# A four-layer state-space block between two mixtures of experts: small arithmetic off GpSimd, skip term on TensorE, packed expert remainders, one delta buffer

## The reference

```python
def ffn(x):                       # E = 8 experts, F = 344, the best K = 2 of them count
    topk_w, topk_idx = top_k(x @ Ws + bs, 2)
    combine = sum(one_hot(topk_idx, 8) * softmax(topk_w)[..., None], axis=1)
    h = silu(einsum('td,edf->tef', x, Wg)) * einsum('td,edf->tef', x, Wu)
    return einsum('ted,te->td', einsum('tef,efd->ted', h, Wd), combine)

def mamba_block(x, p):            # 256 inner channels d, 16 states s
    xp, z = split(rmsnorm(x, p.norm_w) @ p.Win)
    xc = silu(causal_depthwise_conv(xp, p.conv_w, p.conv_b))     # 4 taps
    dt, Bm, Cm = split(xc @ p.Wx)
    delta = softplus(dt @ p.Wdt + p.bdt)
    h[t] = exp(delta[t] * A) * h[t-1] + delta[t] * xc[t] * Bm[t]  # for each d, s
    y = sum_s(h * Cm) + xc * p.Dp                                 # the skip term is xc * Dp
    return x + (y * silu(z)) @ p.Wblk

x = x + 0.5 * ffn(layernorm(x))                                   # "FFN of kind 1"
x = x + (four mamba_blocks of layernorm(x)) @ Wout + bout
x = x + 0.5 * ffn(layernorm(x))                                   # "FFN of kind 2"
```

## Time and profile before

| | |
|---|---|
| time, median of 3 runs | 4565.08 us (4559.62 to 4566.4) |
| profiled execution, first to last instruction | 4554.2 us; no time beyond this span is given for it, and the median is 10.9 us more |
| POOL busy | 4093.5 us (90%) |
| DVE busy | 4047.9 us (89%) |
| PE busy | 3939.2 us (86%), mean granted clock 0.951 |
| ACT busy | 3342.2 us (73%) |
| chain that ended last | POOL 41%, issue 16%, DVE 14%, PE 12%, ACT 8%, DMA 3% |

### The profile page before, as it was taken

One profiled execution on the slowest core, in us unless ns is written; L12 is line 12 of the kernel. 1 busy time (PEld: TensorE's weight loads), 2 busy tenths in 40 slices (PEclk: granted clock), 3 DMA queues, 4 the chain that ended last, 5 costly groups with the idle time before them and its releaser, 6 DMA issues.

```text
span 4554.2 us, 48397 instructions
## 1 busy us (share of the span) xinstructions
PE 3939.2 (86%) x11712; PEld 1280.3 (28%) x11712; DVE 4047.9 (89%) x5505; ACT 3342.2 (73%) x5047; POOL 4093.5 (90%) x1804
## 2 busy tenths in 40 slices
PE   7886777998999999899998999999899989678769
PEld 2221222232322323232232323223232323122223
DVE  2668898999999999999999999999999999889963
ACT  4566776777777777777778777777777777667734
POOL 0559999999999999999999999999999999999960
PEclk9897887999999999999999999999999999789969
DMA  2233544354434444544454445444444554444410
GB/s 72 61 78 95 115 106 98 85 118 110 97 87 112 107 93 99 114 104 96 98 112 96 97 101 119 95 97 101 112 92 89 117 113 91 101 99 95 99 41 5
DMA packets 154562, 434.46 MB, mean 95 GB/s; under 512 B 16429, under 2 KB 53230, under 8 KB 153903
## 3 DMA queue, kind: packets, MB, share of 16 engines
q1 hardware_dynamic: 154287, 431.36, 41.4%
HBM read 150.28 MB, written 12.58 MB: 36 GB/s over the span
## 4 chain that ended last, share of the span: by engine, by line
POOL 41%; issue 16%; DVE 14%; PE 12%; ACT 8%; DMA 3%; SPq 2%; DVEq 0%; ACTq 0%; POOLq 0%
POOL work L909 21%; POOL work L900 19%; DVE work L720 5%; DVE dA_ps L720 4%; SPq L363 2%; PE d_ps L434 2%; PE s_ps L481 2%; DVE work L725 2%; DMA bc_sb<-bc_rows 2%; ACT sg_sb L583 2%; ACT L583 1%; PE b_ps L427 1%; ACT dA_ps L556 1%; DMA dd_sb<-dd_src 1%; ACT L584 1%
## 5 line engine op out<-in xcount | busy, mean ns | idle before, releaser
L909 POOL TENSOR_TENSOR work<-dd_sb,bc_sb 128x2048 f32<-128x2048 f32 x512 | 2319.6, 4531 | 72.4 <-DMA dd_sb<-dd_src 72.2
L556 ACT ACTIVATE dA_ps<-dd_sb,a_sb 128x512 f32<-128x512 f32 x2048 | 1369.2, 684 | 643.1 <-DVE work L725 542.9
L900 POOL TENSOR_TENSOR work<-work,bc_sb 128x1024 f32<-128x1024 f32 x704 | 1655.9, 2359 | 35.1 <-DVE work L720 34.7
L720 DVE TENSOR_TENSOR_SCAN work<-dA_ps,work 128x512 f32<-128x512 f32 x1408 | 1646.7, 1203 | 40.7 <-POOL work L909 32.0
L720 DVE TENSOR_TENSOR_SCAN dA_ps<-dA_ps,work 128x512 f32<-128x512 f32 x640 | 780.9, 1220 | 10.9 <-ACT dA_ps L556 5.1
L434 PE MATMUL d_ps<-sg_sb,wd_sb 128*128 128x512 f32 (+1 forms) x1536 | 721.0, 601 | 18.8 <-DVE sg_sb L805 18.8
L405 PE MATMUL y_ps<-work,sel_sum 128*32 128x512 f32 x4096 | 580.3, 640 | 81.9 <-POOL work L900 53.7
L421 PE MATMUL a_ps<-xT_sb,wg_sb 128*128 128x512 f32 (+1 forms) x768 | 439.5, 655 | 87.1 <-ACT sg_sb L583 80.7
L421 PE MATMUL b_ps<-xT_sb,wg_sb 128*128 128x512 f32 (+1 forms) x768 | 434.5, 648 | 92.2 <-ACT sg_sb L583 87.8
L725 DVE TENSOR_TENSOR work<-dA_ps,bc_sb 128x512 f32<-128x512 f32 x640 | 435.8, 681 | 8.3
L427 PE MATMUL a_ps<-xs_sb,wu_sb 128*128 128x512 f32 (+1 forms) x768 | 412.2, 619 | 20.7 <-DVE sg_sb L805 16.2
(11 more groups left out here) (116 smaller groups left out, 3823.6 us busy)
## 6 DMA issues: line engine op xcount, KB each, us to landing
dd_sb<-dd_src SPq DMA_DIRECT2D x512, 512.0 KB, 8.5
bc_sb<-bc_rows SPq DMA_DIRECT2D x256, 512.0 KB, 5.8
xr_sb<-in_L_attn_x SPq DMA_DIRECT2D x16, 256.0 KB, 3.3
bc_rows<-dbc_sb SPq DMA_DIRECT2D x128, 32.0 KB, 1.7
x<-xr_sb SPq DMA_DIRECT2D x16, 256.0 KB, 3.6
xr_sb<-x SPq DMA_DIRECT2D x16, 256.0 KB, 2.9
out<-xr_sb SPq DMA_DIRECT2D x16, 256.0 KB, 2.3
wg_sb<-in_L_ffn_Wg SPq DMA_DIRECT2D x1, 1376.0 KB
```

Source lines behind the costliest of these rows:

```text
L556: act.activation(dA_ps[:, g % NDA, :], dd_sb[:, b, c, 0, :], ACT.Exp, scale=a_sb[:, l, b, j, c:c + 1]).then_inc(dA_ready, 1)
L720: dve.tensor_tensor_scan(dA if on_dve(i) else tile, dA, tile, 0.0, ALU.mult, ALU.add).then_inc(scanned, 1)
L900: pool.tensor_tensor(work[:, g % RING], work[:, g % RING], bc_sb[:, j, 0, :].unsqueeze(1).broadcast_to([128, 2, T]), ALU.mult).then_inc(po ...
L909: pool.tensor_tensor(work[:, g % RING:g % RING + 2].rearrange("p h c t -> p (h c) t"), dd_sb[:, b, :, 1, :], bc_sb[:, j, 1, :].unsqueeze(1 ...
```

## The change

- **POOL** keeps `dbu` and products only. The layernorm's power becomes Ln and Exp on ACT, and the rest of the small arithmetic goes to DVE. `bn_sb`, `mv_sb` and `rs_sb` become double.
- **`DVE_UNITS`** has six units in place of five, so DVE makes 12 products a phase and POOL 10 pairs in place of 11.
- **The skip term** becomes a matmul of `xc` with a diagonal matrix `ddiag_sb`, the first to write `y_ps` for its half. `y_sb` goes; the product with silu(z) is written over `zs_sb`.
- **Expert remainders.** The last 88 rows of F of four experts, padded to 96, lie together in three tiles. Experts 0 and 4 have two tiles and the others three, 22 to an FFN in place of 24. `xs_sb` becomes double, and `u` of a packed tile is four matmuls of 32 columns.
- **`dd_src`** has one buffer for both halves. `sp1` (the Abs of `b` = 1) waits for the landing of the four DMAs of `b` = 0, and `sp0` for those of `b` = 1 of the phase before.
- **All tables** have other ticks.

```diff
-FT = [(0, 128), (128, 128), (256, 88)]
-NFT = len(FT)
+PACK, PIECE = 4, 32
+NFT, GT = 3, 11
...
-CORE = {"exp": -10, "scan": -1, "dbu": -3, "dve_prod": 0, "pool_prod": 21, "sum": 30, "y0": 87, "y1": 8}
-PREP = {"dc1": 79, "dc0": 65, "sq": -15, "ms": -10, "rms": -10, "xn": 2, "xp0": 15, "conv0": 17, "xp1": 25, "conv1": 25,
-        "silu_xc": 27, "z0": 35, "zc0": 27, "z1": 44, "zc1": 43, "silu_z": 59, "wx": 41, "dbc": 40, "rows": 4, "dt0": 48,
-        "sp0": 48, "delta0": 55, "du0": 59, "dt1": 75, "sp1": 72, "delta1": 79, "du1": 82, "dd0": 49, "dd1": 86, "bc": 52}
-NEAR = {"dc1": 98, "dc0": 84, "sq": 14, "ms": 25, "rms": 24, "xn": 27, "xp0": 45, "conv0": 42, "xp1": 47, "conv1": 53,
-        "silu_xc": 59, "z0": 69, "zc0": 60, "z1": 72, "zc1": 67, "silu_z": 91, "wx": 76, "dbc": 75, "rows": 48, "dt0": 77,
-        "sp0": 77, "delta0": 84, "du0": 84, "dt1": 84, "sp1": 86, "delta1": 93, "du1": 101, "dd0": 71, "dd1": 109, "bc": 55}
-POST = {"x1": 8, "wblk": 83, "h": 91, "attn": 105, "x2": 105}
-POST_NEAR = {"x1": -65, "wblk": 17, "h": 14, "attn": 35, "x2": 56}
-FFN_AT = {"gb": 5, "xs": 2, "g0": 5, "g1": 10, "g2": 10, "burst": 5, "u0": 10, "u1": 17, "u2": 21, "hh0": 13, "hh1": 16,
-          "hh2": 21, "down": 28}
-START = {"load": -130, "bn": -60, "nb": -44, "xtok": -54, "xt": -38, "xT": -47, "lg": -32, "lg_sb": -35, "mx": -32,
-         "mi": -28, "gap": -17, "we": -31, "eq": -27, "den": -17, "inv": -27, "comb": -13, "ct": -12, "gates": -19}
-END = {"yt": 21, "xo": 32, "bn": 41, "nb": 62, "xtok": 61, "ht": 84, "h": 74, "store": 133, "acc": 10}
+CORE = {"exp": -9, "scan": -1, "dbu": -24, "dve_prod": 2, "pool_prod": 11, "sum": 31, "y0": 90, "y1": 9}
+PREP = {"dc1": 84, "dc0": 51, "sq": -15, "ms": -6, "rms": -8, "xn": 3, "xp0": 17, "conv0": 13, "xp1": 21, "conv1": 22,
+        "silu_xc": 27, "z0": 101, "zc0": 96, "z1": 112, "zc1": 105, "silu_z": 123, "wx": 35, "dbc": 36, "rows": 25, "dt0": 38,
+        "sp0": 40, "delta0": 47, "du0": 52, "dt1": 67, "sp1": 77, "delta1": 82, "du1": 84, "dd0": 11, "dd1": 112, "bc": 71}
+NEAR = {"dc1": 103, "dc0": 78, "sq": 9, "ms": 24, "rms": 19, "xn": 27, "xp0": 46, "conv0": 46, "xp1": 55, "conv1": 54,
+        "silu_xc": 59, "z0": 120, "zc0": 111, "z1": 121, "zc1": 117, "silu_z": 123, "wx": 65, "dbc": 61, "rows": -6, "dt0": 67,
+        "sp0": 69, "delta0": 76, "du0": 76, "dt1": 93, "sp1": 96, "delta1": 106, "du1": 107, "dd0": 45, "dd1": 117, "bc": 65}
+POST = {"x1": 37, "wblk": 92, "h": 93, "attn": 108, "x2": 106}
+POST_NEAR = {"x1": -37, "wblk": 15, "h": 11, "attn": 60, "x2": 59}
+FFN_AT = {"gb": 6, "xs": 4, "g0": 5, "g1": 8, "g2": 10, "burst": 5, "u0": 11, "u1": 13, "u2": 16, "hh0": 13, "hh1": 15,
+          "hh2": 21, "down": 34}
+START = {"load": -130, "bn": -50, "ln": -53, "rs": -52, "nb": -45, "xtok": -47, "xt": -37, "xT": -42, "lg": -37, "lg_sb": -34, "mx": -34,
+         "gap": -34, "mi": -34, "we": -36, "eq": -33, "den": -34, "inv": -34, "w1": -33, "eqw": -30, "comb": -28, "hi": -27,
+         "rest": -24, "mid": -20, "lo": -19, "ct": -14, "gates": -23}
+END = {"yt": 36, "xo": 35, "bn": 37, "ln": 39, "rs": 39, "nb": 49, "xtok": 58, "ht": 81, "h": 78, "store": 133, "acc": 3}
...
-DVE_UNITS = (0, 2, 3, 5, 6)
+DVE_UNITS = (0, 1, 3, 5, 6, 7)
...
+def tiles_of(e):
+    return range(0 if e % PACK else 1, NFT)
+def tiles_until(x):
+    return GT * (x // PACK) + max(0, NFT * (x % PACK) - 1)
+def tile_number(x, ft):
+    return tiles_until(x) + (ft if x % PACK else ft - 1)
+def owner(e, c):
+    return e - e % PACK + (4 * (e % PACK - 1) + c) // 3
 def job_bank(x, job):
-    return "ab"[(7 * x + job) % 2]
+    return "ab"[(2 * tiles_until(x) + x + job) % 2]
...
+        ddiag_sb = sb("ddiag_sb", [128, NL, NBLK, 128])
...
-        dd_src = sb("dd_src", [128, NBLK, 2, T])
+        dd_src = sb("dd_src", [128, 2, T])
...
-        xs_sb = sb("xs_sb", [128, T])
+        xs_sb = sb("xs_sb", [128, 2, T])
...
+                    if j == 0:
+                        pe.wait_ge(xc_ready, 2 * k + b + 1)
+                        pe.matmul(y_ps[:, :], ddiag_sb[:, PHASE[w][1], b, :], xc_sb[:, w % 2, b, :],
+                                  start=True, stop=False).then_inc(y_skip, 1)
                     for c in range(NG):
                         g = HALVES * k + 2 * u + c // 2
                         last = pe.matmul(y_ps[SEL * c:SEL * (c + 1), :], sel_sum[:, :], work[:, g % RING, c % 2, :],
-                                         start=(j == 0), stop=(j == NJ - 1))
+                                         start=False, stop=(j == NJ - 1))
                     last.then_inc(summed, 1)
...
+                    if (at := EXPERT_OF.get(t - FFN_AT[f"u{ft}"])) and ft in tiles_of(at[1]):
                         f, e = at
-                        ps = fill(job_bank(E * f + e, 4 + ft), hh_ready, NFT * (E * f + e) + ft + 1)
-                        pe.wait_ge(xs_ready, E * f + e + 1)
-                        pe.matmul(ps[0:fn, :], wu_sb[:, e, f0:f0 + fn], xs_sb[:, :], start=True, stop=True).then_inc(u_full, 1)
+                        x = E * f + e
+                        ps = fill(job_bank(x, u_job(x, ft)), hh_ready, tile_number(x, ft) + 1)
+                        pe.wait_ge(xs_ready, x + 1)
+                        if ft == 0:
+                            for c in range(NG):
+                                last = pe.matmul(ps[PIECE * c:PIECE * (c + 1), :],
+                                                 wu_sb[:, tile_number(e, ft), PIECE * c:PIECE * (c + 1)],
+                                                 xs_sb[:, owner(e, c) % 2, :], start=True, stop=True)
+                            last.then_inc(u_full, 1)
+                        else:
+                            pe.matmul(ps[:, :], wu_sb[:, tile_number(e, ft), :], xs_sb[:, e % 2, :], start=True, stop=True).then_inc(u_full, 1)
...
+                    for ft in tiles_of(e):
+                        pe.wait_ge(hh_ready, tile_number(E * f + e, ft) + 1)
+                        last = pe.matmul(d_ps[:, :], wd_sb[:, tile_number(e, ft), :], sg_sb[:, ft, :], start=(tile_number(e, ft) == 0),
...
+            def log_act(what, f):
+                m = NORM_OF[what, f]
+                act.wait_ge(mv_done, m + 1)
+                if m > 1:
+                    act.wait_ge(xtok_ready, m - 1)
+                act.activation(rs_sb[:, m % 2, 0, :], mv_sb[:, m % 2, :, 1], ACT.Ln, bias=eps_sb[:, 0:1]).then_inc(var_log, 1)
+
+            def rstd_act(what, f):
+                m = NORM_OF[what, f]
+                act.wait_ge(var_log, m + 1)
+                act.activation(rs_sb[:, m % 2, 0, :], rs_sb[:, m % 2, 0, :], ACT.Exp, scale=-0.5).then_inc(rstd_done, 1)
...
-                            act.wait_ge(y_gated, 2 * (before - 1) + b + 1)
+                            act.wait_ge(wblk_full, before)
...
-                        if k > 0:
-                            act.wait_ge(dd_loaded[b], 64 * k)
-                        act.activation(dd_src[:, b, 0, :], s_ps[:, :], ACT.Abs).then_inc(sp_abs, 1)
+                        if b == 1:
+                            act.wait_ge(dd_loaded[0], 64 * (k + 1))
+                        elif k > 0:
+                            act.wait_ge(dd_loaded[1], 64 * k)
+                        act.activation(dd_src[:, 0, :], s_ps[:, :], ACT.Abs).then_inc(sp_abs, 1)
...
-                    par, l = w % 2, PHASE[w][1]
+                    par = w % 2
                     dve.wait_ge(summed, UNITS * k + NJ * (b + 1))
-                    dve.scalar_tensor_tensor(y_ps[:, :], xc_sb[:, par, b, :], dp_sb[:, l, b:b + 1], y_ps[:, :],
-                                             ALU.mult, ALU.add).then_inc(y_skip, 1)
-                    dve.wait_ge(y_skip, 2 * k + b + 1)
                     dve.wait_ge(zs_ready, 2 * k + b + 1)
-                    if k > 0:
-                        dve.wait_ge(wblk_full, k)
-                    dve.tensor_tensor(y_sb[:, b, :], zs_sb[:, par, b, :], y_ps[:, :], ALU.mult).then_inc(y_gated, 1)
+                    dve.tensor_tensor(zs_sb[:, par, b, :], zs_sb[:, par, b, :], y_ps[:, :], ALU.mult).then_inc(y_gated, 1)
...
+                    if xn > 1:
+                        dve.wait_ge(u_full, tile_number(xn - 1, 1))
+                    dve.tensor_tensor(xs_sb[:, e % 2, :], xT_sb[:, f % 2, :], ps_of[job_bank(xn, 0)][:, :], ALU.mult).then_inc(xs_ready, 1)
...
+                dve.scalar_tensor_tensor(rs_sb[:, m % 2, 1, :], mv_sb[:, m % 2, :, 0], -1.0, rs_sb[:, m % 2, 0, :], ALU.mult, ALU.mult).then_inc(nb_ready, 1)
...
+                if (f := UNIT_OF.get(t - START["gap"])) is not None:
+                    dve.wait_ge(mx_ready, f + 1)
+                    if f > 0:
+                        dve.wait_ge(we_ready, f)
+                    dve.tensor_tensor(wt_sb[:, 0, :], mx_sb[:, :, 1], mx_sb[:, :, 0], ALU.subtract).then_inc(gap_ready, 1)
...
+                if (f := UNIT_OF.get(t - START["eqw"])) is not None:
+                    dve.wait_ge(rt_step, 4 * f + 3)
+                    dve.wait_ge(eq_ready, f + 1)
```

(22 more changed lines are left out.)

224 lines of the change are left out of this document (103 added, 121 removed).

## The result

The changed kernel takes 5190.31 us (median of 4 runs, 5152.34 to 5192.91) against 4562.35 us before in the same session (4557.17 to 4566.4). The ratio is 1.1359, 95% interval 1.1322 to 1.1396: 628 us slower, where 130 were forecast. The profiled execution spans 5190.4 us.

The account below looks back on a forecast made before the run. POOL bounds the kernel before; after the change DVE does, stalled by the one delta buffer: 50.3 + 17.5 + 0.5 us make 68.3 a phase. Stretches of +112, +26, +7 and -15 give +130, so 4695 us (4640 to 4770; 8 in 10: 4430 to 4770).

Parts of the forecast that it names:

- The sum: Whole kernel: phases of 68.3 us in the middle, in all +130 us on the profiled span, to 4684 us.
- the stall at `delta`: DVE's queue at `delta1`: DVE stands still for 4.9 us in each phase, waiting for the one buffer's chain.
- DVE's other waits: Waits left in the rest of DVE's loop: 0.5 us a phase, bounds 0 and 1.9.
- Small arithmetic at 0.185 us each: Router and norm steps moved to DVE, priced like the 32-column comparison: 0.9 us a phase in all.
- the third rival: DVE instructions with two SBUF tensors wait for POOL's long ones, 272 by 1.6 us: 435 us, 5130 us in all; chance 0.06.
- The sign that I named for it: In the profile after: DVE idle ahead of small instructions of 0.2 us would show that POOL and DVE exclude each other.
- The one delta buffer: Chain from `du0` over ACT, four DMAs and `sp1` to `delta1`: 17.5 us, said to decide the outcome.
- the 12.6 us of cover: DVE's queued work from tick 52 to 81, set against the 17.5 us chain; called the step most likely to fail.
- Costs set at nothing: `bc` loads, `dbu` one unit ahead, ACT's bank free two ticks later, `z` over `zs_sb`: no cost each.
- `z` over `zs_sb`: ACT's `z` waits for `wblk` at tick 92 of the same window, four ticks ahead in the order: no cost.
- POOL's 59.8: POOL's work after the change: 59.8 us a phase, from 63.9 before.
- POOL sets the pace: Kernel before, middle: POOL busy 97.7% sets the pace of 65.4 us a phase, DVE 1.1 us behind.

Follow-up runs that it names:

- m1: Small kernel of its own: POOL's products of 2048 columns beside eight kinds of DVE instruction; one with two SBUF inputs of four columns took 3.08 us, 0.16 with POOL done.
- e1: The changed kernel with the router's small steps (not comparison, reciprocal) and the norm's last step back on POOL: 5003.5 us, 1.0958 of before.
- e3: The changed kernel with small arithmetic back on POOL and two delta buffers, skip diagonal of layer 0 everywhere: 4794.7 us, 1.0501 of before.
- e2: The changed kernel with two delta buffers and layer 0's skip diagonal in all layers: 5010.6 us, 1.0974 of before.
- e4: e3 with the queue places of the kernel before wherever they could be had: 4695.5 us, 1.0288 of before.
- e9: e6 with START's and END's norm places of the kernel before: 4653.9 us, 1.0209 of before.
- e6: e4 with the norm's reciprocal root on POOL (EPS, power) in place of ACT's Ln and Exp: 4696.7 us, 1.0290 of before.
- b4: b3 with `y_sb` and all places of `z` back, the other moved places kept: 4668.9 us, 1.0225 of before.
- b3: The kernel before with `z` late, y's product over `zs_sb`, no `y_sb`, and some places around them moved: 4743.4 us, 1.0385 of before.
- e12: e9 with all 24 tiles unpacked, one `xs_sb`, and the skip term back on DVE: 4734.5 us, 1.0380 of before.
- v1: The kernel before with the norm's EPS and power moved from POOL to ACT's Ln and Exp: 4583.8 us, 1.0052 of before.
- b2: The kernel before with six units in `DVE_UNITS` in place of five: 4610.1 us, 1.0103 of before.

## Why the prediction was wrong, step by step

- **The sum.** The terms account for the difference between the forecast and the measured phase (middle, us a phase): DVE's own work 62.5 for 62.9, -0.4; small instructions held by POOL, +4.4; the stall at `delta` 2.8 for 4.9, -2.1; DVE's other waits 6.2 for 0.5, +5.7. Together +7.6, which is 75.9 for 68.3, and over 64 phases 486 of the 506 us by which the span exceeds the forecast's 4684.
- **Small arithmetic at 0.185 us each** is the step that failed first. The price came from an instruction that ran while POOL stood still, as the prediction itself noted under the third rival. The rival's mechanism is right: m1 shows it by itself, and e1 and e3 price it at 187 to 216 us, the few moved places of their edit included. Its size was not: it held all 272 for 1.6 us, 435 us. In the middle four lines of the router and norm are held, and the others run in POOL's gaps. The sign that I named for it was wrong too: DVE is not idle ahead of these instructions, they are longer themselves. The rival's total of 5130 us lies closer to the result than mine, but in part by chance, since it left out the order. The Trainium skill states the rule (SBUF — State Buffer, section Who interferes with whom) also for cast and `tensor_scalar` in VectorE's two-port modes, and says that whoever comes first holds the ports for a whole instruction. For DVE the runs agree: in m1 both forms last until POOL's instruction ends, 2.1 us on average. For POOL they show only that it waits too: 1.0 us over four instructions (19.21 for 18.2), where each of DVE's takes 0.69 by itself. A chance of 0.06 for a mechanism that the prediction had worked out, and against which no row spoke, was too low.
- **The one delta buffer.** The chain is right: DVE behind ACT's Ln, ACT behind the DMAs, and its length, 17.9 us for 17.5. That PE waits for `dc` behind it was not forecast. The stall of 4.9 us a phase was mis-sized: 2.8 by the waits, 2.8 to 3.3 by e2 and e3. The step that failed is the 12.6 us of cover, and in the way that the prediction named: it counted DVE's work, and 2.0 us of waits lie between, so that DVE came to `delta1` later.
- **Costs set at nothing** failed most. The new order as a whole had no term. The places that e4 and e9 move back cost 141 us (4794.7 to 4653.9, e3 to e9; the norm's root goes back to POOL on the way, worth 1 us in e6), and those that stay cost 103 (b4). The 141 were measured with the small instructions on POOL, whose wait for DVE's reciprocal falls from 142.6 us in e3 to 64.4 in e9, so that a part of them may be a price of the edit of e3; what the order costs in the changed kernel as it is, no run shows. `z` over `zs_sb`, of which I wrote only that its wait stands four ticks ahead in the order, costs 74 (b3 against b4). I read the wait's place but not how long ACT waits for a `z` between `y` and the next phase's start: 141.3 us for 30.4.
- **The other terms.** POOL's 59.8 (59.0) and DVE's 62.9 (62.5) were right, and packing and the skip pay 81 us. PE's work was 63.6 us a phase, not 59, at a granted clock of 0.91 for 0.99; PE is not the busiest engine, but DVE waits for it, and no run shows what the lower clock adds to these waits.
- **The balance** of 628 us, step by step: held small instructions and the delta buffer 396; the places moved back in e4 and e9 141; the other moved places 103 and the late `z` 74; six units, double statistics and the rest together nothing (e12 against b3, by the ratio); packing and skip -81. That is 633; the medians of before move by 8 us between sessions. The rows of this sum depend on the order in which the parts are taken away: six units cost 47 in the kernel before, and in e12 nothing together with the other small parts.
- **POOL sets the pace** is itself half true. v1 takes 0.95 us a phase off POOL and loses 21 us; b2 takes 2.4 off POOL, gives DVE 1.2 to 1.4 more and loses 47. In both POOL's wait for DVE's scans grows, from 24.7 us to 62.5 and 177.7. With two engines at 97.7 and 96.0%, relief of the first was worth nothing here; why v1 is slower and not only as fast is not shown.

## What to carry to other kernels

Before small arithmetic moves from POOL to VectorE, ask for each instruction what else POOL does at that time: with two SBUF inputs, or a cast or `tensor_scalar` from SBUF to SBUF, 0.16 us became the rest of POOL's instruction here; read one input from PSUM, or place it where POOL waits. In a kernel whose queues were laid out by hand, cost a buffer taken away by the place that its writer is pushed to, and do not set the new order at nothing: moving five operations of a window by 2 to 4 ticks cost about 100 us here without any change of work. A term at nothing that covers a whole table needs a range of its own.

## What the runs showed of the hardware

- A held VectorE instruction is shown as busy, not as waiting: 3958 ns mean for a cast of 32 columns that takes 171 ns at L950.
- The hold works both ways: POOL's four products took 19.21 us beside DVE's 512-column products, and 18.22 to 18.24 in the other stages of m1.
- Reciprocal, MAX8, a product with one input in PSUM and a scan with one input in PSUM were not held beside POOL (0.18, 0.17, 0.19 and 1.22 us in m1).
- The chain over the four `dd` DMAs took 17.5 to 18.3 us in each of 39 phases; its length as worked out in the prediction, mostly from an idle part of the program, is 17.5.
